# Three attention and combine stages of a four-layer network: division, output and normalisation at other ticks, and copies by ScalarE

## The reference

```python
x = x + _L0_xattn_ref(_layernorm(x), ctx_2048, ctx_2048, ...)   # 16 heads, rotary, output matrix Wm
x = x + _L0_ffn_ref(_layernorm(x), ...)
x = x + _L1_xattn_ref(_layernorm(x), ctx_2048, ctx_2048)        # 8 heads, no matrices
x = x + _L1_ffn_ref(_layernorm(x), ...)                         # 32 experts, 6 per row, 48 places each, and a shared one
x = x + _L2_xattn_ref(_layernorm(x), ctx_2048, ctx_2048, ...)   # 32 query heads, 8 key heads, output matrix Wfc
x = x + _L2_ffn_ref(_layernorm(x), ...)
x = x + _L3_xattn_ref(_layernorm(x), ctx_2048, ...)
x = x + _L3_ffn_ref(_layernorm(x), ...)
```

## Time and profile before

| | us |
|---|---|
| median of 3 runs | 2837.04 (2834.32 to 2837.44) |
| the profiled execution, its own time | 2834.09 |
| its span, first to last instruction | 2832.3 |
| attention of layer 0 | about 12 to 314 |
| combine of layer 1, first addition to its end | 848 to 928 |
| attention of layer 2 | 929 to 1172 |

### The profile page before, as it was taken

One profiled execution on the slowest core, in us unless ns is written; L12 is line 12 of the kernel. 1 busy time (PEld: TensorE's weight loads), 2 busy tenths in 40 slices (PEclk: granted clock), 3 DMA queues, 4 the chain that ended last, 5 costly groups with the idle time before them and its releaser, 6 DMA issues. The chain is left out here.

```text
span 2832.3 us, 45749 instructions
## 1 busy us (share of the span) xinstructions
PE 2294.6 (81%) x14565; PEld 1665.8 (59%) x14574; DVE 1838.1 (65%) x3821; ACT 1516.0 (54%) x3393; POOL 1499.8 (53%) x1491
## 2 busy tenths in 40 slices
PE   4898244978988487599279999976999997999998
PEld 2333022547545243487257777755888886788886
DVE  4777585755546255355478888866788885666565
ACT  0767383752120156344368888865878874344443
POOL 5542105510000443286078888836888884788883
PEclk9999665989999589799689999988999998999999
DMA  5242103532040433242300000011000000344443
GB/s 137 65 97 65 50 0 91 159 104 111 1 184 1 92 70 88 66 120 77 110 1 1 0 0 0 1 45 42 6 4 6 4 1 18 104 110 116 115 111 87
DMA packets 119445, 174.20 MB, mean 62 GB/s; under 512 B 25597, under 2 KB 79005, under 8 KB 116207
## 3 DMA queue, kind: packets, MB, share of 16 engines
q1 hardware_dynamic: 118703, 171.58, 21.4%
q10 hardware_dynamic: 576, 0.52, 0.1%
HBM read 122.06 MB, written 11.48 MB: 47 GB/s over the span
## 5 line engine op out<-in xcount | busy, mean ns | idle before, releaser
L526 DVE TENSOR_REDUCE a_mraw<-a_wave_ps 128x4 f32<-128x1024 f32 (+1 forms) x256 | 308.1, 1218 | 125.2 <-PE a_wave_ps L358 122.4
L414 ACT ACTIVATE a_et<-a_wave_ps 128x1024 f32<-128x1024 f32 x256 | 262.5, 1027 | 137.8 <-PE a_wave_ps L375 134.5
L2937 POOL TENSOR_SCALAR a3o_raw<-a3o_raw,a3o_mu,a3o_dev 128x128 f32<-128x128 f32 x320 | 305.2, 966 | 5.6 <-issue 5.6
L2937 POOL TENSOR_SCALAR a3x_raw<-a3x_raw,a3x_mu,a3x_dev 128x128 f32<-128x128 f32 x320 | 280.2, 888 | 4.8 <-issue 4.8
L146 POOL TENSOR_TENSOR row_rstd<-row_var,row_half 128x14 f32<-128x14 f32 (+6 forms) x15 | 26.1, 1740 | 378.4 <-DVE row_var L141 378.4
L1752 DVE TENSOR_TENSOR f3e_hidden_low<-f3e_hidden,f3e_hidden_high 128x512 fp32r<-128x512 f32 x96 | 115.9, 1207 | 126.4 <-ACT f3e_hidden_high L1705 125.9
L392 PE MATMUL a_o_ps<-a_et,a_vt 128*32 128x256 f32 x2048 | 169.8, 404 | 18.8 <-ACT a_osb L444 17.2
L1613 POOL TENSOR_TENSOR f3e_product<-f3e_silu,f3e_up 128x512 f32<-128x512 f32 x96 | 143.4, 1497 | 73.0 <-PE f3e_u_ps L1632 46.0
L358 PE MATMUL a_wave_ps<-a_ks,a_qs 64*128 64x256 bf16 (+2 forms) x1280 | 121.1, 266 | 25.3 <-DMA a_ks<-a_parts 11.5
L1698 ACT ACTIVATE f3e_silu<-f3e_g_ps 128x512 f32<-128x512 f32 x96 | 57.4, 598 | 144.1 <-PE f3e_g_ps L1632 137.1
L2928 POOL TENSOR_TENSOR a3o_dev<-a3o_var,a3o_minus_half 128x24 f32<-128x24 f32 x16 | 68.8, 4303 | 118.0 <-DVE a3o_var L3228 118.0
(11 more groups left out here) (483 smaller groups left out, 6847.8 us busy)
## 6 DMA issues: line engine op xcount, KB each, us to landing
f_w<-in_f_w SPq DMA_DIRECT2D x16, 1216.0 KB, 8.7
a_qs<-a_parts SPq DMA_DIRECT2D x144, 128.0 KB, 2.4
f_raw<-in_f_w SPq DMA_DIRECT2D x60, 256.0 KB, 2.7
a_ks<-a_parts SPq DMA_DIRECT2D x96, 128.0 KB, 2.4
f3e_spread<-f3e_shares SPq DMA_DIRECT2D x64, 192.0 KB, 3.0
f2e_spread<-f2e_shares SPq DMA_DIRECT2D x36, 256.0 KB, 3.3
f3e_spread<-f3e_shares SPq DMA_DIRECT2D x64, 128.0 KB, 3.1
f_raw<-in_f_w SPq DMA_DIRECT2D x60, 128.0 KB, 2.7
```

The costliest lines, as they stand in the source:

```text
L414: self.nc.scalar.activation(self.et[:, g % self.WAVES_HELD, :, :], self.wave_ps[:, self.second_place[g][0], :, :], ACT.Exp, scale=self.sca ...
L526: v.tensor_reduce(out, wave.rearrange("p u (c n) -> p u c n", n=N), AX.X, ALU.max).then_inc(self.max_taken, 1)
L2937: mm = nc.gpsimd.tensor_scalar(head, head, mu[:, h:h + 1], dev[:, h:h + 1], ALU.subtract, ALU.mult)
```

## The change

*Attention class*: a parameter out (14 by default) sets OUT = DONE + out, the tick of output product and addition; statistics follow at OUT + 2. *Layer 0*: out = 15, one tick later; the division stays at DONE + 13 but stands ahead of sum and shift in GpSimd's order (both fall into the same tick of a pair). *Layer 2*: LEAD 14 in place of 18, out = 18 (OUT stays at tick 53), the division at OUT - 1 (tick 52 as before); SP writes four slots per tick at ticks 8 to 10; pairs from the second on are normalised two ticks earlier (6 - 2W = -2); the bias is added to X at tick 8 in place of 0, and with it goes the wait for the constants; ScalarE waits for the presets only ahead of its first copy into v. *Combine*: six PSUM banks in rotation; ScalarE copies each of the first twelve batches' banks to SBUF, GpSimd adds high and low part to X, four batches an instruction; the last group is added by VectorE as before; the statistics come at the comparisons 9 to 12 of the next group.

```diff
+        self.OUT = self.DONE + out
-        return range(self.W * (B - 2) + self.DONE + 17)
+        return range(self.W * (B - 2) + self.OUT + 3)
@@ layer 0
-                      stacks=3, values=4)
+                      stacks=3, values=4, out=15)
+                    if (q := a.pair_at(g, DONE + 13)) is not None:
+                        a.pool_divide(pool, q)
                     if (q := a.pair_at(g, 14)) is not None:
                         pool.wait_ge(k_taken, 2 * q + 2)
...
-                    if (q := a.pair_at(g, DONE + 13)) is not None:
-                        a.pool_divide(pool, q)
@@ tensor and vector
-                    if (q := a.pair_at(g, DONE + 14)) is not None:
+                    if (q := a.pair_at(g, OUT)) is not None:
@@ layer 2
-        a = Attention(nc, st, rows, "a2", heads=32, width=8, n=128, halves=2, scale=1.0 / float(np.sqrt(8.0)), lead=18,
-                      stacks=4, values=5)
+        a = Attention(nc, st, rows, "a2", heads=32, width=8, n=128, halves=2, scale=1.0 / float(np.sqrt(8.0)), lead=14,
+                      stacks=4, values=5, out=18)
-                        if (q := a.pair_at(g, 8 + i)) is not None:
+                        if (q := a.pair_at(g, 8 + i // 2)) is not None:
                             slot(q, i)
-                    if (q := a.pair_at(g, 0)) is not None:
+                    if (q := 0 if g == 0 else a.pair_at(g, 6 - 2 * W)) is not None:
                         wait(pool, x_done, q)
                         for u in range(2):
                             a.pool_normalise(pool, 2 * q + u, xn[:, u, :])
+                    if (q := a.pair_at(g, 8)) is not None:
                         pool.wait_ge(a.xn_ready, 2 * q + 2)
                         pool.wait_ge(a.consts_in, 16 * len(loads))
-                    if (q := a.pair_at(g, DONE + 13)) is not None:
+                    if (q := a.pair_at(g, OUT - 1)) is not None:
                         a.pool_divide(pool, q)
@@ scalar
-                act.wait_ge(a.preset, a.presets())
...
+                        if q == 0:
+                            act.wait_ge(a.preset, a.presets())
@@ combine
-                out_ps = ct.ps("out_ps", [P, 4, 512])
+                BANKS, HELD = 6, B - 4
+                out_ps = ct.ps("out_ps", [P, BANKS, 512])
+                kept = ct.sb("kept", [P, HELD, 2 * D])
-                                    wait(pe, added, 4 * (tb - 1) + t + 1)
-                                mm = nc.tensor.matmul(out_ps[:, t, :], back[:, q % 2, t * P:t * P + P],
+                                    wait(pe, kept_out, 4 * tb + t - BANKS + 1)
+                                mm = nc.tensor.matmul(out_ps[:, (4 * tb + t) % BANKS, :], back[:, q % 2, t * P:t * P + P],
-                            if tb > 0 and q < 4:
-                                rows.dve_stats(4 * (tb - 1) + q)
...
+                            if tb > 0 and 8 <= q < 12:
+                                dve.wait_ge(added, tb)
+                                rows.dve_stats(4 * (tb - 1) + q - 8)
...
+                        for b in range(HELD):
+                            act.wait_ge(summed, Q * (b // 4) + Q)
+                            nc.scalar.copy(kept[:, b, :], out_ps[:, b % BANKS, :]).then_inc(kept_out, 1)
...
+                        for tb in range(HELD // 4):
+                            k = slice(4 * tb, 4 * tb + 4)
+                            pool.wait_ge(kept_out, 4 * tb + 4)
+                            nc.gpsimd.tensor_tensor(X[:, k, :], X[:, k, :], kept[:, k, 0:D], ALU.add).then_inc(high_added, 1)
+                            pool.wait_ge(high_added, tb + 1)
+                            nc.gpsimd.tensor_tensor(X[:, k, :], X[:, k, :], kept[:, k, D:2 * D], ALU.add).then_inc(added, 1)
```

More of the change, by code:

```diff
@@ L186, with __init__ @@
     RING = 3
-    def __init__(self, nc, st, rows, name, heads, width, n, halves, scale, lead, stacks, values):
+    def __init__(self, nc, st, rows, name, heads, width, n, halves, scale, lead, stacks, values, out=14):
         self.nc, self.st, self.rows, self.X, self.name = nc, st, rows, rows.X, name
@@ L491, in pool_deviation @@
     def pool_deviation(self, pool, g):
-        if (q := self.pair_at(g, self.DONE + 16)) is not None and q >= B // 2 - 2:
+        if (q := self.pair_at(g, self.OUT + 2)) is not None and q >= B // 2 - 2:
             if q == B // 2 - 2:
@@ L501, in dve_rows @@
     def dve_rows(self, dve, g):
-        if (q := self.pair_at(g, self.DONE + 16)) is not None:
+        if (q := self.pair_at(g, self.OUT + 2)) is not None:
             dve.wait_ge(self.added, q + 1)
@@ L2612, in _ @@
                                                     ALU.is_equal).then_inc(back_ready, 1)
-                            if tb > 0 and q < 4:
-                                rows.dve_stats(4 * (tb - 1) + q)
-                            if q == Q - 1 and tb == 3:
-                                rows.dve_variance(dve, 0, 12)
-                            if q == Q - 1:
-                                dve.wait_ge(summed, n + 1)
-                                for t in range(4):
-                                    x = X[:, tb * 4 + t, :]
-                                    nc.vector.tensor_tensor(x, x, out_ps[:, t, 0:D], ALU.add)
-                                    nc.vector.drain()
-                                    nc.vector.tensor_tensor(x, x, out_ps[:, t, D:2 * D], ALU.add).then_inc(added, 1)
-                                dve.wait_ge(added, 4 * tb + 4)
@@ L2625, in _ @@
-                        for b in range(12, B):
-                            rows.dve_stats(b)
-                        rows.dve_variance(dve, 12, B)
+                            if tb > 0 and 8 <= q < 12:
+                                dve.wait_ge(added, tb)
+                                rows.dve_stats(4 * (tb - 1) + q - 8)
+                            if n == 4 * Q - 1:
+                                rows.dve_variance(dve, 0, HELD)
+                        dve.wait_ge(summed, 4 * Q)
+                        for b in range(HELD, B):
+                            x, k = X[:, b, :], b % BANKS
+                            nc.vector.tensor_tensor(x, x, out_ps[:, k, 0:D], ALU.add)
+                            nc.vector.drain()
+                            nc.vector.tensor_tensor(x, x, out_ps[:, k, D:2 * D], ALU.add)
@@ L2629, in _ @@
+                        nc.vector.drain()
+                        for b in range(HELD, B):
+                            rows.dve_stats(b)
+                        rows.dve_variance(dve, HELD, B)
+                    @block.scalar
+                    def _(act):
+                        for b in range(HELD):
+                            act.wait_ge(summed, Q * (b // 4) + Q)
+                            nc.scalar.copy(kept[:, b, :], out_ps[:, b % BANKS, :]).then_inc(kept_out, 1)
                     @block.gpsimd
@@ L2636 @@
+                        rows.pool_deviation(pool, 1, 0, HELD)
+                        rows.pool_deviation(pool, 2, HELD, B)
 HEAD = 128
```

10 lines of the change are left out of this document (5 added, 5 removed).

## The result

The changed kernel takes 2805.7 us (median of four, 2804.5 to 2809.3) beside 2837.24 for the kernel before: a ratio of 0.988 (95% interval 0.985 to 0.991). It lies inside the predicted range of 2775 to 2808, but 12.7 us above the predicted time. A second set on the chip gave 2800.0 beside 2840.1, a ratio of 0.986 (0.984 to 0.988). The forecast was 44 us less than before; the two sets measured 32 and 40 less.

A forecast was written before the change was run, and what follows sets the result against it. Stages run one after another, each bound by the engine it waits for; 16 (combine) + 7 (layer 0) + 21 (layer 2) = 44 us off the profiled 2834.1 gives 2790, as a median 2793; range 2775 to 2808.

The forecast's parts named there:

- Part 1: Combine of layer 1: each of three boundaries costs 0.5 us in place of 5.9, 16 us gained (14.5 to 17).
- Part 2: Layer 0's attention: earlier division brings a pair to 29.0 us, 6 us; output product's tick 1.1; together 7 (2 to 11).
- Part 3: Layer 2's attention to tick 40: later preset wait and earlier normalisation gain 11.0 us, less 0.3 for four wave ticks: 10.7.
- Part 4: Layer 2, ticks 40 to 72: SP's order closes a loop of 21.5 us a pair, 86 for four: 4.4 us lost.
- rival A: Layer 2, ticks 40 to 72: SP keeps up, loop not closed, 72 to 75 us; whole 2779 to 2782; chance 0.22.
- Part 5: Layer 2 after tick 72: 15 ticks without slots gain 12 us, the output product 3 more; tail as long as before.
- B: Layers 2 and 0: slots come too late for a pair's first wave; whole 2801 to 2810; chance 0.15.
- C: Layer 2, same SP order: slower than before if a pair takes more than 32.5 us; chance 0.03.
- D: Combine boundaries stay and layer 0's division waits as the sum did; only layer 2's start gains: 2817 to 2830; chance 0.04.

The follow-up runs named there:

- e_l0_div: The kernel before with only layer 0's division moved ahead of the sum, output product's tick unchanged: 2833.6 us, ratio 0.998.
- e_act_maxima: The full change, but in layer 2's attention ScalarE instead of SP issues the transfer of the maxima, behind its own copy: 2791.8 us, ratio 0.983.
- e_l2_start: The kernel before with only layer 2's later wait for the presets (bias at tick 8) and normalisation two ticks earlier, lead 18 kept: 2820.0 us, ratio 0.993.

## Why the prediction was right, and where it was not

*Part 1, the combine*: right, 3 x (5.9 - 0.5) = 16 and 16.0 measured. The eight profiles with the edit have 62.6 to 62.7 us, the five without 78.6 to 78.8.

*Part 2, layer 0*: right. 28.9 us a pair for 29.0, and the stage 7.0 us shorter (mean of eight profiles with the edit, 308.0, of four without, 315.0). e_l0_div with the division alone ended at 309.7, 0.2 above what was expected of it: 5 us for the division, 2 for the output product, where I had 6 and 1. The spread lands nearer to its issue than 3.16 us: the last of four is issued at about 153.8 and the division starts at 156.25.

*Part 3, layer 2 up to tick 40*: 7.6 and 9.4 us for 10.7. Up to the fourth transposition of a normalised pair it fits (8.75 for 8.9 in the first profile: 63.8 us before, 55.1 after). What failed is "four more ticks of waves lie before this point and cost perhaps 0.3": from there to tick 40 the full change took 35.9 and 37.0 us, the two kernels that kept lead 18 and SP's issue 33.7 and 33.8. That is 2 to 3 us, not 0.3. The slots' wait of 2.2 us (3.9 in the second profile), which no term had, lies ahead of that transposition; before, the wave found its slots there.

*Part 4, ticks 40 to 72*: right in mechanism, and in size by two terms that offset. 86.2 us for 86.0, a loss of 4.6 for 4.4 (2.8 in the second profile). But it was not 4 x 21.5: from the turn at 999.42 to the waves that waited at 1022.36, 1044.90 and 1067.32 it is 22.9, 22.5 and 22.4 us, 1 us more than 21.5. SP needed 17.5 for the odd maxima's issue and the 23 behind it, so 16.85 for the 23 where I took 16.2; the 1.86 us ahead of it I had at 1.7, and my own terms add up to 21.7, not 21.5. The slow pace of 0.77 us was misread as well: the 19.3 us of the earlier trace rows hold 1.4 us in which SP waited for the even maxima, and a pair has 26 transfers, not 25. Without that wait the pace is 0.72, or 16.5 for 23. The last of the four pairs is shorter, 18.3 from there to the turn of tick 72, since the fourth wait stands just behind that turn. e_act_maxima opened the loop and got 76.7, just above the 72 to 75 of rival A. The estimate that TensorE alone needs about 72 was right: 73.3 and 71.9 in the two kernels with lead 18.

*Part 5, after tick 72*: 9.5 and 10.8 us for 15. The step that failed is "now 15 ticks remain, without slots on SP: 24.4 us, and 1 for odd waits". To the last wave it was 29.75. The fourth wait for even maxima, at 1089.61, falls here: their transfer stood behind the slots of the last pair, issued before tick 72. It is 3.74 us and the low clock behind it, about the 4.3 us by which 29.75 exceeds 25.4. The output product gave its 3 (2.7: 4.7 us from the last wave to the last store where it was 7.4), but the tail behind the store was not "as long as before": 20.5 for 19.4 us. GpSimd's statistics, 2.6 us long, ran into the time when the last division could start, where before it they had been done 3.4 us earlier:

```profile
1130.39 2.61 POOL L146 TENSOR_TENSOR row_rstd<-row_var,row_half 128x14 f32<-128x14 f32 x1 [6.36 <-DVE row_var L141]
1132.98 1.26 POOL L457 TENSOR_TENSOR a_on<-a_oc,a_zr 128x512 f32<-128x512 f32 x1
```

In the second profile they didn't, and the tail was 19.3.

By this accounting layer 2 gave 12.5 us in the first profile and 14 in the mean of three, where 21 stood: 7 to 8.5 of the 12.7 us missing. The rest lies in the untouched stages, and whether all of it is scatter isn't settled.

*The rivals.* A, SP keeps up, was refuted as a forecast and shown as a possibility: with the maxima off SP, the middle is 10 us shorter. The Trainium skill (DMA: Bandwidth & Descriptors, section "Issuing engines are not separate DMA queues") says that issuing from several engines saves only the sequencer's time, usually small beside the transfer. The trace agrees as far as one issue goes (0.6 us); here it differs where 23 of them stand ahead of a transfer on which TensorE waits: moving two of a pair's 26 transfers took 14 us off the stage against the first profile and 9 against the second. B, the slots too late, has the time range in which the first set's result fell (2801 to 2810), but it is half the story: the slots cost 7.1 us of waiting in four places, the maxima 12.0, and with the maxima gone and the slots' waits left the stage had 218.2. C asked for 32.5 us a pair; none was seen. D is out.

What stays open: how the shorter lead's loss divides between SP's order and the first slots. Lead 18 changes both. That lead 14 with ScalarE's issue has the shortest stage of all (218.2, beside 220.7 and 222.1 at lead 18) speaks for SP's order, one profile each. Two pairs of slots a tick at lead 18 may be worth 3 us (220.7 against 223.7), within the scatter. Which of the edits in e_l2_start carries how much wasn't run.

## What to carry to other kernels

Shortening a pipeline's lead moves every transfer's place in an issuing queue that is nearly full: write down the order of the queue for one period, and count what stands ahead of each transfer that somebody waits for, also in the periods in which the queue's own work has ended. Make small edits one at a time where a bundle mixes them: here the earlier normalisation and the later wait for the presets (with the bias out of the way) carried the stage's gain, and the shorter lead cost a part of it. Price a short wait of TensorE that recurs at more than its length, by the clock behind it. Compare stages over several profiles before a stage that was not touched is said to have paid.

## What the hardware showed that I had not expected

The issue of a transfer isn't one price: mostly 0.60 us for a slot, 0.4 for one row of 256 B, 0.61 on ScalarE's own stream, and for a few of a stage's 96 slots 1 to 2.4 us, twice even 3.8 and 3.9, with nothing else changed. Some stages have two lengths in single executions: 232 and 236 us for layer 1's experts, one in each of the full change's two profiles. And short gaps cost clock: of the twelve waits of 2.1 us for the normalisation in the middle of the four kernels that keep layer 2's old attention, eleven were followed by a stretch at 1.2 GHz, while the waits of 1.5 us for the maxima there were not. With gaps of 1.8 to 4.6 us once a pair the granted clock was 0.90 in the mean, without them 1.00, and about the same products took 7 us less.
